# Three PSUM banks for Q in the edge stage, half of a pair's Q rows made a step sooner, and digit products and relu pair by pair

## The reference

```python
Q, K, V = x @ Wq, x @ Wk, x @ Wv              # 8 heads of 64
score = einsum('ehd,ehd->eh', K[src], Q[dst]) / 8
score = exp(clip(score, -5, 5))
wV = segment_sum(V[src] * score, dst)
Z  = segment_sum(score, dst)
h  = x + wV / (Z + 1e-6)
h  = batch_norm(h) * gamma + beta             # over the nodes
out = layer_norm(x + h)                        # over the 512
```

## Time and profile before

| | |
|---|---|
| median of three runs | 2119.94 us |
| the profiled execution | 2113.25 us |
| its span, first to last instruction | 2111.5 us |
| TensorE busy | 1918.3 us, 91% |
| VectorE busy | 1696.9 us, 80% |
| ScalarE busy | 1377.7 us, 65% |
| GpSimd busy | 1249.1 us, 59% |
| the edge stage | about 460 to 1967 us |

### The profile page before, as it was taken

One profiled execution on the slowest core, in us unless ns is written; L12 is line 12 of the kernel. 1 busy time (PEld: TensorE's weight loads), 2 busy tenths in 40 slices (PEclk: granted clock), 3 DMA queues, 4 the chain that ended last, 5 costly groups with the idle time before them and its releaser, 6 DMA issues.

```text
span 2111.5 us, 41623 instructions
## 1 busy us (share of the span) xinstructions
PE 1918.3 (91%) x7904; PEld 1351.1 (64%) x8014; DVE 1696.9 (80%) x2454; ACT 1377.7 (65%) x4602; POOL 1249.1 (59%) x1473
## 2 busy tenths in 40 slices
PE   7999999989998998998899899898899899899887
PEld 4555555547776776776677677676676677677433
DVE  6676655538888888888888888888888888888988
ACT  0001000018887887887888888788788788788866
POOL 0106663026666666666666666666666666666657
PEclk9999999999999999999999999999999999999999
DMA  4648886358998898888888989898899899889607
GB/s 172 176 147 299 293 301 237 143 206 300 315 326 291 304 322 307 313 305 309 306 307 305 325 315 311 301 314 300 296 321 309 294 317 320 307 300 331 225 0 289
DMA packets 184521, 589.09 MB, mean 279 GB/s; under 512 B 28480, under 2 KB 30240, under 8 KB 184480
## 3 DMA queue, kind: packets, MB, share of 16 engines
q0 software_dynamic: 135904, 465.14, 63.5%
q1 hardware_dynamic: 45120, 121.69, 16.2%
q10 hardware_dynamic: 3456, 1.78, 0.3%
HBM read 535.27 MB, written 78.91 MB: 291 GB/s over the span
## 4 chain that ended last, share of the span: by engine, by line
PE 70%; DVE 16%; issue 7%; another core or an unknown queue 2%; ACT 2%; DMA 1%; POOL 1%; SPq 0%; DVEq 0%; ACTq 0%; POOLq 0%
PE q_ps L915 26%; PE places L342 20%; PE acc L940 19%; DVE kv L791 11%; PE mm_ps L925 2%; DVE stats L1278 1%; DVE agg L1262 1%; ACT agg L1189 1%; DVE raw L802 1%; PE mm_ps L927 1%; DVE agg L1271 1%; PE places L402 1%; PE banks L1132 1%; DMA kv<-kv_d,idx 1%
## 5 line engine op out<-in xcount | busy, mean ns | idle before, releaser
L747 POOL DMA_INDIRECT kv<-kv_d,idx x880 | 891.9, 1014 | 548.9 <-issue 214.0
L842 ACT ACTIVATE kv<-kv 128x64 f32<-128x64 f32 x3520 | 888.9, 335 | 14.3
L940 PE MATMUL acc<-kv,mm_sb 128*128 128x260 f32 x3520 | 852.1, 385 | 11.9 <-issue 4.4
L940 PEld LDWEIGHTS acc<-kv,mm_sb 128*128 128x128 f32 x3520 | 672.8, 192 | 114.3 <-issue 10.7
L791 DVE TENSOR_TENSOR kv<-q_ps,kv 128x1024 f32<-128x1024 f32 x440 | 536.4, 1219 | 214.7 <-PE q_ps L915 161.1
L915 PE MATMUL q_ps<-q_tile,mm_sb 128*128 x1760 | 550.0, 434 | 146.0 <-DVE kv L791 114.7
L802 DVE TENSOR_REDUCE raw<-kv 128x16 f32<-128x1024 f32 x440 | 532.7, 1211 | 0.0
L915 PEld LDWEIGHTS q_ps<-q_tile,mm_sb 128*128 128x128 f32 x1760 | 316.9, 190 | 285.3 <-DVE kv L791 193.6
L852 ACT ACTIVATE mm_sb<-mm_ps,less 128x1024 fp32r<-128x1024 f32 x220 | 241.5, 1098 | 66.2 <-remote 60.1
L710 DVE TENSOR_TENSOR kv<-kv 128x384 f32<-128x384 f32 (+1 forms) x440 | 271.8, 618 | 0.0
L856 ACT ACTIVATE kv<-raw 128x16 f32<-128x16 f32 x440 | 92.0, 209 | 197.9 <-DVE raw L795 181.8
(11 more groups left out here) (171 smaller groups left out, 1354.1 us busy)
## 6 DMA issues: line engine op xcount, KB each, us to landing
q_tile<-q_d SPq DMA_DIRECT2D x49, 512.0 KB
kv<-kv_d,idx POOLq DMA_INDIRECT x880
kv_d<-kv_a SPq DMA_DIRECT2D x25, 512.0 KB
xb<-in_x POOLq DMA_DIRECT2D x49, 256.0 KB, 4.2
xb_d<-xb POOLq DMA_DIRECT2D x49, 256.0 KB, 3.7
out_rows<-agg SPq DMA_DIRECT2D x49, 256.0 KB, 2.1
x_sb<-in_xT SPq DMA_DIRECT2D x24, 512.0 KB, 8.1
q_d<-q_a SPq DMA_DIRECT2D x24, 512.0 KB
```

Source lines behind the costliest of these rows:

```text
L747: pool.indirect_dma_start(kv[:, s, u, 0:2 * DIM], None, kv_d, bass.IndirectOffsetOnAxis(idx[:, s, u:u + 1], 0), bounds_check=N_NODES - 1, ...
L842: return act.activation(v, v, ACT.Copy, scale=kv[:, s, u, 2 * DIM + h:2 * DIM + h + 1])
L940: last = pe.matmul(acc[:, bass.ds(par, 1), DIM - (1 - n) * HALF:DIM + n * HALF], m, kv[:, sc, u, DIM + n * HALF:DIM + (n + 1) * HALF], sta ...
```

## The change

`q_ps` gets a third bank. An even pair uses banks 0 and 1, an odd pair banks 1 and 2. The visit whose bank the pair before does not use (visit 0 of an even pair in bank 0, visit 1 of an odd pair in bank 2) is computed at the end of step q for pair q+2 (`soon`); the other one, in bank 1, is computed at the start of step q for pair q+1 (`late`) and its first matmul waits for `s_mul` as before. `s_qx` still rises once per pair, after the late visit. The bank comes from `mm_ps`, which shrinks to one bank with one pair in it. Digit products and relu are done for one pair in every step; the products of pair q+4 wait for the relu of pair q+3, and the relu in ScalarE's step q waits for the products of pair q+4. `s_t` and `s_mm` are still shared by two slots and so count two per round (`of_two`). The registers that hold the tile of each visit are filled a step sooner.

```diff
-        mm_sb = sb("mm_sb", [P, RING // 2, 2, 4 * P], F32R)
+        mm_sb = sb("mm_sb", [P, RING, 2, 2 * P], F32R)
-        mm_ps = ps("mm_ps", [P, 2, 4 * P], F32)
-        q_ps = ps("q_ps", [P, 2, DIM], F32)
+        mm_ps = ps("mm_ps", [P, 2, 2 * P], F32)
+        q_ps = ps("q_ps", [P, 3, DIM], F32)
+        def of_two(s, fills):
+            return 2 * fills - 1 + s % 2
...
-                    dve.tensor_tensor(k, q_ps[:, :, :], k,
+                    dve.tensor_tensor(k, q_ps[:, s % 2:s % 2 + 2, :], k,
...
-                if s % 2 == 0 and there(a):
-                    act.wait_ge(s_t[sa // 2], fa)
+                if there(a):
+                    act.wait_ge(s_t[sa // 2], of_two(sa, fa))
                     wait(act, s_seg[sa], fa - 1)
-                    wait(act, s_seg[sa + 1], fa - 1)
-                    act.activation(mm_sb[:, sa // 2, :, :], mm_ps[:, :, :], ACT.Relu,
+                    act.activation(mm_sb[:, sa, :, :], mm_ps[:, :, :], ACT.Relu,
...
+            def rows_of(sb_, u, tile):
+                for n in range(2):
+                    part_q = q_tile[:, bass.ds(tile % 2, 1), n * DIM:(n + 1) * DIM].bitcast(F32R)
+                    m = pe.matmul(q_ps[:, sb_ % 2 + u, :], one_hot(sb_, u, 1), part_q, start=(n == 0),
+                                  stop=(n == 1))
+                    if n == 0:
+                        first_m = m
+                return first_m, m
...
                 if there(b):
+                    late = 1 - sb_ % 2
+                    tile = pe.snap(tile_regs[(2 * sb_ + late) % PLACES], min_val=0, max_val=TILES - 1)
+                    if late == 1:
+                        pe.wait_ge(s_q, 16 * (tile + 1))
+                    first_m, last = rows_of(sb_, late, tile)
+                    if there(q):
+                        first_m._wait_ge(s_mul[s], multiplied)
+                    last.then_inc(s_qx, 1)
+                if there(a):
+                    pe.wait_ge(s_lb[sa // LB_PAIRS], 16 * fa)
+                    m1, f1 = at(s, fills, 3)
+                    wait(pe, s_mm[m1 // 2], of_two(m1, f1))
+                    for u in range(2):
+                        pe.matmul(mm_ps[:, 0, u * P:(u + 1) * P], lb[:, sa, u * P:(u + 1) * P], nb[:, :], start=True,
+                                  stop=True)
+                    pe.matmul(mm_ps[:, 1, :], nb[:, :], lb[:, sa, :], start=True, stop=True).then_inc(s_t[sa // 2], 1)
...
+                if there(d):
+                    soon = sd % 2
...
+                    pe.wait_ge(s_mm[sd // 2], of_two(sd, fd))
+                    pe.wait_ge(s_q, 16 * (tiles[soon] + 1))
+                    rows_of(sd, soon, tiles[soon])
```

More of the change, by code:

```diff
@@ L696, in follow @@
             return regs, fetch, bit
+        def of_two(s, fills):
+            return 2 * fills - 1 + s % 2
         def one_hot(s, u, by_node):
-            n = 2 * (s % 2) + u
-            return mm_sb[:, s // 2, by_node, n * P:(n + 1) * P]
+            return mm_sb[:, s, by_node, u * P:(u + 1) * P]
         def heads(ap):
@@ L896, in _ @@
             pe.wait_ge(s_nb, 16)
+            def rows_of(sb_, u, tile):
[6 more added lines that the diff above has]
+                return first_m, m
             def step(q, s, fills):
-                a, b, c = q + 4, q + 1, q - 2
@@ L900, in step @@
-                (sa, fa), (sb_, fb), (sc, fc) = at(s, fills, 4), at(s, fills, 1), at(s, fills, -2)
+                a, b, c, d = q + 4, q + 1, q - 2, q + 2
+                (sa, fa), (sb_, fb), (sc, fc), (sd, fd) = (at(s, fills, 4), at(s, fills, 1), at(s, fills, -2),
+                                                           at(s, fills, 2))
                 if there(b):
-                    tiles = []
-                    for u in range(2):
[L904 to L928, removed]
+                    late = 1 - sb_ % 2
@@ new lines, in step @@
+                    tile = pe.snap(tile_regs[(2 * sb_ + late) % PLACES], min_val=0, max_val=TILES - 1)
+                    multiplied = fills if isinstance(fills, int) else pe.to_reg(fills)
+                    if late == 1:
[8 more added lines that the diff above has]
+                    wait(pe, s_mm[m1 // 2], of_two(m1, f1))
+                    for u in range(2):
+                        pe.matmul(mm_ps[:, 0, u * P:(u + 1) * P], lb[:, sa, u * P:(u + 1) * P], nb[:, :], start=True,
+                                  stop=True)
+                    pe.matmul(mm_ps[:, 1, :], nb[:, :], lb[:, sa, :], start=True, stop=True).then_inc(s_t[sa // 2], 1)
@@ L943, in step @@
                     last.then_inc(s_seg[sc], 1)
-                if s == RING - 1:
+                if there(d):
+                    soon = sd % 2
+                    tiles = []
+                    for u in range(2):
+                        v = 2 * sd + u
+                        tile = pe.snap(pe.snap(tile_regs[(v - 1) % PLACES], min_val=0, max_val=TILES - 1)
+                                       + bit((2 * s + 2 + u) % VBODY), min_val=0, max_val=TILES - 1)
+                        pe.reg_mov(tile_regs[v % PLACES], tile)
+                        tiles.append(tile)
+                    pe.wait_ge(s_mm[sd // 2], of_two(sd, fd))
+                    pe.wait_ge(s_q, 16 * (tiles[soon] + 1))
+                    rows_of(sd, soon, tiles[soon])
+                if s == RING - 2:
                     fetch(q // RING + 2 if isinstance(q, int) else fills + 1)
```

## The result

Median of four runs: 2150.24 us after (2143.62 to 2152.61) against 2119.32 us before (2116.89 to 2123.97), ratio 1.0147 [1.0118, 1.0175]. Forecast: 2056 us. The profiled execution took 2152.61 us, its span is 2150.8 us.

A forecast was written before the change was run, and what follows sets the result against it. It took a TensorE-VectorE loop through the single-pair `q_ps` as the bound: 163 us to gain, cut by the DMA share to 64 us, other terms nothing, so 2119.94 - 64 = 2056 us. Range 2000 to 2165 us.

The forecast's parts named there:

- The loop: TensorE's Q rows and VectorE's product wait for each other through `q_ps`; two pairs go from 6.65 to 5.91 us.
- The added register instructions: On TensorE, about three more per pair, 0.2 us, hidden behind matmuls; between nothing and 88 us, taken as nothing.
- the signs asked for: TensorE's waits for the product and VectorE's for Q rows under 50 us each; DMA share 0.92 or more.
- From there to the product that reads them 1.04 us: In the two-pair loop, from the end of Q rows to VectorE's product; 0.33 us after the other group.
- the split: Digit products and relu pair by pair: same TensorE work, 0.22 us off the loop; relu's 62 us on ScalarE hidden.
- relu rival: Single digit-product bank: a late relu holds up TensorE's next products and sums, 57 and 40 us exposed; chance 0.11.
- The transfers' cap: DMA share rises from 0.89 only to 0.93, so a pair takes 3.244 us and the gain is 64 us.
- the best 16 us: Highest DMA share seen in the profile, 0.95 at 339 GB/s; if held, a gain of 94 us.
- Relu's price: On ScalarE, a relu of 512 elements takes 0.69 us; two instead of one add 0.14 us a pair, hidden.
- Code: TensorE's loop body grows some 35 instructions, ending near slot 509 of 512; rival: no longer resident, 2195 us, chance 0.11.
- The single bank's 2153 us: Rival: relus behind evictions (57 us) and doubled relu waits (+40) hold up TensorE, added to 2056 us; chance 0.11.
- The late visibility grows: Rival: VectorE sees TensorE's Q rows later, 2120 to 2256 us; chance 0.08 for no change, 0.06 for slower.

The follow-up runs named there:

- a_direct_b: Changed kernel with every indirect gather replaced by a direct DMA of fixed rows, chip C: 1912.3 us, 0.9111 of the kernel before.
- b_direct_b: Kernel before with every indirect gather replaced by a direct DMA of fixed rows, chip C: 1901.34 us, 0.906 of the kernel before.
- after3: The changed kernel as it is, run again on chip C: 2113.68 us against 2098.24 for the kernel before, ratio 1.0064.
- b_mm1_b: Kernel before with only digit products and relu pair by pair in one bank, Q as before, chip C: 2130.51 us, 1.0145 of the kernel before.
- c_third: Kernel before with only the third bank and early visit (one-hot matrices wrong, work the same), chip E: 1907.62 us, 0.998 of the kernel before.
- b_fixed_b: Kernel before with indirect gathers kept but indices made by counting, so fixed rows are read, chip F: 1910.38 us, 1.0011 of the kernel before.
- b_mm1: Kernel before with only digit products and relu pair by pair in one bank, Q as before, chip D: 1928.79 us, 1.010 of the kernel before.
- a_mid: Changed kernel with relu moved into the middle of ScalarE's weighings and digit products behind the sums, chip B: 2144.88 us, 1.0149 of the kernel before.
- after2: The changed kernel as it is, run again on chip B: 2148.28 us against 2112.94 for the kernel before, ratio 1.015.
- b_fixed: Kernel before with indirect gathers kept but indices made by counting, so fixed rows are read, chip E: 1910.15 us, 1.0002 of the kernel before.

## Why the prediction was wrong, step by step

- **The loop: the steps were right, their cause was not.** A group of four Q matmuls, digit products and sums takes what was reckoned: with prompt completions a_direct_b's steps are 2.92 and 2.93 us long (Q rows at 1196.05, 1198.97 and 1201.90 us of its span), where 2.9 was said, and digit products of one pair take 1197.40 - 1197.17 = 0.23 us. But the kernel before, with its two banks, does 2.92 us a pair as well once nothing is late (b_direct_b), and its Q rows hardly wait for the product (9.6 us). What stretched a pair to 3.39 us was the late completions in the loop, not the single-pair buffer by itself. The added register instructions, priced at nothing to 88 us, are in a_direct_b's steps as well, which are on average 0.03 us longer in all. Of the signs asked for, TensorE's waits for the product did fall under 50 us each (26.1 and 47.9). VectorE's for Q rows did not (95.3, and 136.2 for nothing visible), and the DMA share stayed under 0.92.
- **The step that failed: "From there to the product that reads them 1.04 us" was "kept as a term".** It is no constant of the loop but what one completion happened to be late. Half of the sums' completions were late, by 1.8 us, in before already. The third bank, which was to take 64 us (163 without the transfers) out of a loop with this constant in it, gives 17 on chip C (after3 against b_mm1_b) and 2 to 3 us where nothing is late (c_third).
- **The second: the split was priced at nothing, twice.** "In every step instead of every second it is the same work for TensorE": on chip D, with nothing late and TensorE busy over 99%, it costs 18 us. "From nothing to the price of the relu rival below; I take nothing, since ScalarE reaches that relu about a step before TensorE needs it": a step of room is 2.9 us, and the relu waited up to 4.5 us for a late completion. Measured, the split is +32 us on chip C. 32 - 17 = +15 us; on the first chip the sum was +31, and its parts were not measured apart there. With prompt completions two undisturbed pairs take 1201.90 - 1196.05 = 5.85 us in a_direct_b and 5.82 (1195.62 to 1201.44) in b_direct_b, 440 x 0.015 = 7 us; the other 6 of the 13 us lie in single longer steps that were not traced.
- **The transfers' cap never decided.** The 64 us were drawn from a DMA share of 0.93; it fell from 0.89 to 0.87. In b_direct_b it is 0.99 at 380 GB/s, in the kernel before with fixed rows (b_fixed_b) 1.00 at 379, so the 0.95 of the best 16 us was no ceiling.
- **Relu's price.** 0.674 us was measured, 0.69 reckoned. Right, and hidden as a duration.
- **Code.** 18 packets before and after (and 23 in the second instruction queue both times): nothing is fetched in each round. The count was off: in the traces with direct DMAs a round of eight steps has 370 rows of TensorE's matmuls, weight loads and register instructions before and about 386 after, 16 more and not 35. From slot 104 that ends near 490. By the Trainium skill ("Runtime: NRT & Kernel Launch", Instruction fetch mechanics) a taken branch out of the held window would wait for a fetch. This body still lies within the 512 slots of the prediction's count, so the rule was not put to the test.
- **The rivals.** The single bank's 2153 us is the measured 2150 by luck. Its condition came true, TensorE's next digit products waiting for the relu (32.2 us; the 148.0 us of their weight loads for nothing visible are mostly no sign of it, since b_mm1 has 114.3 us of them, 0.29 a time, on a chip where nothing is late, and after 0.37 a time). Its mechanism did not: it was built from relus behind evictions and doubled small waits. The relu waited for TensorE's completion. "The late visibility grows" named that, with its sign (the product's wait for Q rows, visible and not, 95.3 + 136.2 us, though TensorE's is small), but looked for it at VectorE alone. Both played a part, and they were given 0.11 and 0.14 as if apart.
- **Not in the prediction at all: the clock.** An idle TensorE of some us is paid twice, as the windows at 1610 us show. Over four runs after has a mean granted clock of 0.974; the profiled run before has 0.990. I estimate (0.990 - 0.974) x 2150 = 34 us of full clock. The sums' starts give about the same: (1.626 - 1.554) x 440 = 32 us, as much as the whole loss of 31. How much of it lies on the path was not measured: a_mid has a higher clock than after2 (0.983 and 0.975) and takes the same time.

## What to carry to other kernels

A "remote" wait, or an engine idle though its releaser ended long ago, may be a completion that is seen late. It belongs in the sum as a spread of delays that every new consumer meets, not as a constant of a loop. Before a buffer is halved to pay for another, ask how late the event that frees it can be: the relu's waits for nothing visible were 40.4 us with two pairs in hand and 157.6 with one (b_mm1_b). Then ask what the finer pieces cost an engine that is nearly full: here 18 us with nothing late at all. And a verdict of 1 or 2% is one on a chip: the same change was +15 and +31 us on two of them, and its split +18 or +32.

## What the runs showed of the hardware

- The same kernel takes 1910 us on three chips and 2098 to 2119 us in three other comparisons (at least two chips), at mean clocks of 0.995 and 0.989 to 0.990. With direct DMAs in place of indirect ones it takes 1900 and 1901 us on either kind.
- On the slow kind half of TensorE's completions are late while GpSimd issues gathers, and the late ones are seen 0.86 us behind the end of an issue. The gathers' own rows are not longer there: 1014 ns in before, 1041 ns in b_mm1 on chip D (512 to 1700 us):

```profile
L747 POOL DMA_INDIRECT kv<-kv_d,idx x698 | 708.0, 1014 | 351.9 <-issue 170.2 <-remote 170.1 <-PE acc L940 11.1
```

```profile
L749 POOL DMA_INDIRECT kv<-kv_d,idx x797 | 829.6, 1041 | 229.6 <-issue 196.8 <-PE acc L940 19.7 <-ACT kv L857 12.2
```

  With direct DMAs, issued by the same engine in 548 ns each, nothing is late on chip C (b_direct_b). The Trainium skill ("Perfetto Trace Analysis", DMA Instruction — SWDGE (GPSIMD)) says that such a row ends when the last descriptor is written, not when the data have moved; by that rule the 0.86 us are behind the writing of descriptors. That completions and descriptors get in each other's way is argued from this coincidence in time (and the 44 groups due outside, none late) and from the direct runs, not shown; whether the spread of the rows that are read plays a part stays open, since b_fixed met no chip of the slow kind. Why chips differ is open too.
